# Attention in a five-phase kernel: the running maxima are split by GpSimd, transposed into score banks, copied out by ScalarE and added to the query rows by GpSimd

## What is computed

```
q = rope((layernorm(x) @ Wq.T + bq) per head)        # (4, 16, 512, 16)
k = rope((ctx @ Wk.T + bk) per head)
v = (ctx @ Wv.T + bv) per head
attn = softmax(einsum('bhld,bhkd->bhlk', q, k) * 16 ** -0.5, over k)
x = x + tanh(g_xattn[0]) * ((attn @ v) @ Wp.T + bp)
```

## Time and profile before

| | |
|---|---|
| median of 3 runs | 832.74 us (831.04 to 834.12) |
| the profiled execution's own time | 834.48 us |
| its span, first to last instruction | 832.7 us |
| mean granted TensorE clock | 0.932 |
| PE busy | 694.4 us (83%) |
| DVE busy | 475.5 us (57%) |
| ACT busy | 329.4 us (40%) |
| POOL busy | 245.0 us (29%) |
| first matmul of the attention passes to the start of the next phase | 109.3 to 328.0 us |

### The profile page before, as it was taken

The page is one execution under the profiler, slowest core; times in us unless marked ns, Lnnn a source line. Parts: engine busy times, 40 slices in busy tenths (PEclk is TensorE's granted clock), DMA queues, the critical chain, the costliest instruction groups (busy, mean ns, idle before and its releaser), DMA issues. The chain is left out here.

```text
span 832.7 us, 10715 instructions
## 1 busy us (share of the span) xinstructions
PE 694.4 (83%) x3613; PEld 413.5 (50%) x3632; DVE 475.5 (57%) x873; ACT 329.4 (40%) x584; POOL 245.0 (29%) x407
## 2 busy tenths in 40 slices
PE   3699869998998997855799999999488999975886
PEld 1377633333333332742455665656355767662554
DVE  3576668888888871643763113121437555456995
ACT  0167626677677676412341111141031120202565
POOL 2356530011011010353050001010103164347797
PEclk9699977999999999885899999999789998996999
DMA  5010000000000001930000000000100000000011
GB/s 186 13 32 25 13 7 0 2 1 0 1 1 1 1 1 71 394 155 0 1 1 0 1 1 0 0 0 1 13 1 0 1 1 1 1 0 0 20 38 45
DMA packets 14104, 21.45 MB, mean 26 GB/s; under 512 B 2160, under 2 KB 11504, under 8 KB 13296
## 3 DMA queue, kind: packets, MB, share of 16 engines
q1 hardware_dynamic: 13200, 20.34, 7.1%
q10 hardware_dynamic: 864, 0.59, 0.2%
HBM read 18.83 MB, written 2.10 MB: 25 GB/s over the span
## 5 line engine op out<-in xcount | busy, mean ns | idle before, releaser
L630 ACT ACTIVATE prob<-ps_s 128x512 f32<-128x512 f32 x256 | 133.9, 600 | 72.3 <-PE ps_s L518 71.6
L562 DVE TENSOR_REDUCE mx<-ps_f 128x2 f32<-128x1024 f32 x128 | 150.0, 1218 | 15.6 <-PE ps_f L498 8.1
L1038 DVE SCALAR_TENSOR_TENSOR qs<-ps_u,wmax,qs 128x512 f32<-128x512 f32 x40 | 29.7, 749 | 113.9 <-ACT qs L1000 113.8
L1000 ACT ACTIVATE qs<-ps_g,wmax 128x512 f32<-128x512 f32 x40 | 27.4, 687 | 144.1 <-PE ps_u L903 144.1
L916 PE MATMUL ps_yE<-down,qs 128*128 128x256 f32 x320 | 77.7, 387 | 7.9 <-DVE qs L1038 6.8
L518 PE MATMUL ps_s<-q_stacks,k_stacks 64*128 64x512 f32 x256 | 75.7, 425 | 10.2 <-ACT prob L630 9.1
L498 PE MATMUL ps_f<-k_stacks,q_stacks 64*128 64x512 f32 x256 | 64.9, 502 | 16.7 <-DVE q_stacks L581 9.7
L916 PEld LDWEIGHTS ps_yE<-down,qs 128*128 128x128 f32 x320 | 61.3, 193 | 22.0 <-DVE qs L1038 9.0
L527 PE MATMUL ps_o<-prob,vst 128*32 128x512 f32 x512 | 69.0, 612 | 0.0
L498 PEld LDWEIGHTS ps_f<-k_stacks,q_stacks 64*128 64x128 f32 x256 | 25.3, 194 | 72.7 <-issue 28.7
L599 POOL COPY vst<-va 128x272 f32<-128x272 f32 x16 | 6.8, 428 | 167.1 <-PE ps_o L527 167.1
(11 more groups left out here) (245 smaller groups left out, 1258.7 us busy)
## 6 DMA issues: line engine op xcount, KB each, us to landing
up<-in_up SPq DMA_DIRECT2D x10, 256.0 KB, 6.7
x<-in_x SPq DMA_DIRECT2D x4, 512.0 KB, 7.9
ctxT<-in_ctxT SPq DMA_DIRECT2D x16, 128.0 KB, 2.0
ks<-in_ctxTC SPq DMA_DIRECT2D x1, 2048.0 KB, 11.9
ks<-in_ctx SPq DMA_DIRECT2D x1, 2048.0 KB, 17.4
out<-x SPq DMA_DIRECT2D x16, 128.0 KB, 1.7
down<-in_down SPq DMA_DIRECT2D x1, 1280.0 KB, 5.7
ks<-in_wqv SPq DMA_DIRECT2D x1, 1024.0 KB, 20.7
```

Source lines behind the costliest of these rows:

```text
L562: dve.tensor_reduce(mx[:, f % 2, qt, 2 * pair:2 * pair + 2], ps_f[n % 2][:, :, :], AX_X, ALU.max).then_inc(used, 1)
L630: act.activation(prob[:, kt % 2, j, :], ps_s[n % 3][:, :], ACT.Exp, scale=SCALE)\
L1038: dve.scalar_tensor_tensor(out=h[:, k % 2, :], in0=ps_u[k % 2][:, :], scalar=wmax[:, 3, order[k], 1:2], in1=sg[:, k % 2, :], op0=ALU.mult, ...
```

## The change

Four things are changed together, all of them in `phase_attend`.

- The **split** of the maxima leaves VectorE's program and goes to GpSimd's, as three instructions for two (L576, L578 and L580 of the changed kernel). VectorE's program is now the 128 reductions and nothing else, and it no longer waits for the clearing of `mt`.
- The **transposes** go four by four, one half for each pair of heads, into banks of `ps_s` in place of a unit of `ps_f`. They take two places in the order of the score banks, ahead of scores 0 and of scores 2 in kt = 2 of the step before (they stood together at the head of kt = 3). The third bank back is now sometimes one of theirs.
- **ScalarE copies** each transposed half (128 x 512) out of its bank into the new tile `minus`, between its exponentials, and **GpSimd adds** it into the query rows (`lower`, L586, 128 x 512), two such additions per step in place of VectorE's single one.
- The first pass runs **14 units ahead** of the second in place of 12.

```
-def max_unit(f):
-    return UNITS + (UNITS + 1) * f + (MAX_AFTER if f < STEPS - 1 else 0)
+def score_slot(s, kt, j):
+    added = (0, 0, 1 + j // 2, 2)[kt] if s + 1 < STEPS else 0
+    return 2 + (QT * G + 2) * s + G * kt + j + added
+
+def max_slot(f, pair):
+    return score_slot(f - 1, 2, 2 * pair) - 1 if f else pair
...
# PE
-            def maxima(f):
-                n = max_unit(f)
+            def maxima(f, pair):
+                n = max_slot(f, pair)
                 pe.wait_ge(mt_ready, f + 1)
-                wait(pe, used, n - 1)
-                for pair in range(2):
-                    for qt in range(QT):
-                        last = pe.transpose(ps_f[n % 2][:, pair, qt * P:(qt + 1) * P], ...)
-                last.then_inc(filled, 1)
+                wait(pe, slot_read, n - 2)
+                for qt in range(QT):
+                    last = pe.transpose(ps_s[n % 3][:, qt * P:(qt + 1) * P], ...)
+                last.then_inc(slot_done, 1)
...
-            for i in range(UNITS):
-                first_scores(0, i)
-            for i in range(MAX_AFTER):
-                first_scores(1, i)
-            maxima(0)
-            for i in range(MAX_AFTER, 4):
-                first_scores(1, i)
+            for n in range(UNITS + 2):
+                first_scores(n)
+            for pair in range(2):
+                maxima(0, pair)
+            for n in range(UNITS + 2, LEAD):          # LEAD = 14
+                first_scores(n)
             for s in range(STEPS):
-                pe.wait_ge(used, max_unit(s) + 1)
+                pe.wait_ge(lowered, 2 * (s + 1))
                 for kt in range(QT):
-                    if kt == QT - 1 and s + 1 < STEPS:
-                        maxima(s + 1)
                     for half in range(2):
-                        f, i = ahead[2 * kt + half]
-                        if f < STEPS:
-                            first_scores(f, i)
+                        ahead = UNITS * s + LEAD + 2 * kt + half
+                        if ahead < UNITS * STEPS:
+                            first_scores(ahead)
+                        if kt == 2 and s + 1 < STEPS:
+                            maxima(s + 1, half)
                         for j in (2 * half, 2 * half + 1):
                             scores(s, kt, j)
...
# GpSimd
+            def split(f):
+                pool.wait_ge(used, UNITS * (f + 1))
+                ...
+                pool.tensor_scalar(high.bitcast(F32R), mx[:, f % 2, :, :], -1.0, None, ALU.mult).then_inc(mt_half, 1)
+                pool.wait_ge(mt_half, 2 * f + 1)
+                pool.tensor_tensor(low, mx[:, f % 2, :, :], high, ALU.add).then_inc(mt_half, 1)
+                pool.wait_ge(mt_half, 2 * f + 2)
+                pool.tensor_scalar(low, low, -1.0, None, ALU.mult).then_inc(mt_ready, 1)
+
+            def lower(f, pair):
+                pool.wait_ge(slot_read, max_slot(f, pair) + 1)
+                own = qs[:, 2 * f + pair, :]
+                pool.tensor_tensor(own, minus[:, pair, :], own.bitcast(F32), ALU.add).then_inc(lowered, 1)
...
             for s in range(STEPS):
                 if s > 1:
                     stage_values(s, s % 2)
+                if s + 1 < STEPS:
+                    split(s + 1)
+                    for pair in range(2):
+                        lower(s + 1, pair)
                 bias(s)
...
# ScalarE
+            def copy_maxima(f, pair):
+                n = max_slot(f, pair)
+                act.wait_ge(slot_done, n + 1)
+                wait(act, lowered, 2 * (f - 1) + pair + 1)
+                act.copy(minus[:, pair, :], ps_s[n % 3][:, :]).then_inc(slot_read, 1)
...
                 for j in range(G):
-                    n = s * 16 + kt * G + j
+                    n = score_slot(s, kt, j)
+                    if kt == 2 and j % 2 == 0 and s + 1 < STEPS:
+                        copy_maxima(s + 1, j // 2)
```

More of the change, by code:

```diff
@@ L478, in phase_attend @@
         filled, used = sem("filled"), sem("used")
-        mt_preset, mt_half, mt_ready = sem("mt_preset"), sem("mt_half"), sem("mt_ready")
-        s_done, exp_done, pv_done, o_copied = sem("s_done"), sem("exp_done"), sem("pv_done"), sem("o_copied")
+        mt_preset, mt_half, mt_ready, lowered = sem("mt_preset"), sem("mt_half"), sem("mt_ready"), sem("lowered")
+        slot_done, slot_read, pv_done, o_copied = sem("slot_done"), sem("slot_read"), sem("pv_done"), sem("o_copied")
         v_preset, v_ready = sem("v_preset"), sem("v_ready")
@@ L500, in first_scores @@
                 last.then_inc(filled, 1)
-            def maxima(f):
-                n = max_unit(f)
+            def maxima(f, pair):
+                n = max_slot(f, pair)
                 pe.wait_ge(mt_ready, f + 1)
-                wait(pe, used, n - 1)
-                for pair in range(2):
-                    for qt in range(QT):
-                        last = pe.transpose(ps_f[n % 2][:, pair, qt * P:(qt + 1) * P],
-                                            mt[:, f % 2, qt, 2 * pair:2 * pair + 2, :]
-                                            .rearrange("p h r -> p (h r)"), id32)
-                last.then_inc(filled, 1)
+                wait(pe, slot_read, n - 2)
+                for qt in range(QT):
+                    last = pe.transpose(ps_s[n % 3][:, qt * P:(qt + 1) * P],
+                                        mt[:, f % 2, qt, 2 * pair:2 * pair + 2, :]
+                                        .rearrange("p h r -> p (h r)"), id32)
+                last.then_inc(slot_done, 1)
             def scores(s, kt, j):
-                n = s * 16 + kt * G + j
-                wait(pe, exp_done, n - 2)
+                n = score_slot(s, kt, j)
+                wait(pe, slot_read, n - 2)
                 pair, h = divmod(j, 2)
                 pe.matmul(ps_s[n % 3][:, :], ks[rows(h), 2 * s + pair, kt * P:(kt + 1) * P],
-                          qs[rows(h), 2 * s + pair, :], start=True, stop=True).then_inc(s_done, 1)
+                          qs[rows(h), 2 * s + pair, :], start=True, stop=True).then_inc(slot_done, 1)
             def values(s, kt):
-                pe.wait_ge(exp_done, s * 16 + kt * G + G)
+                pe.wait_ge(slot_read, score_slot(s, kt, G - 1) + 1)
                 if kt == 0:
@@ L557, in _ @@
         def _(dve):
-            def first_maxima(f, i):
-                n = score_unit(f, i)
+            for n in range(UNITS * STEPS):
+                f, i = divmod(n, UNITS)
                 qt, pair = divmod(i, 2)
+                if i == 0:
+                    wait(dve, mt_ready, f - 1)
                 dve.wait_ge(filled, n + 1)
@@ L563, in first_maxima @@
                                   ALU.max).then_inc(used, 1)
[L565 to L589, removed]
         @block.gpsimd
@@ L616, in _ @@
             pool.wait_ge(bp_in, 16)
+            split(0)
+            for pair in range(2):
+                lower(0, pair)
             for s in range(STEPS):
@@ L623, in _ @@
         def _(act):
+            def copy_maxima(f, pair):
[3 more added lines that the diff above has]
+                act.copy(minus[:, pair, :], ps_s[n % 3][:, :]).then_inc(slot_read, 1)
             def exps(s, kt):
+                wait(act, pv_done, s * QT + kt - 1)
                 for j in range(G):
[L626 to L629, removed]
+                    n = score_slot(s, kt, j)
+                    if kt == 2 and j % 2 == 0 and s + 1 < STEPS:
+                        copy_maxima(s + 1, j // 2)
+                    act.wait_ge(slot_done, n + 1)
                     act.activation(prob[:, kt % 2, j, :], ps_s[n % 3][:, :], ACT.Exp, scale=SCALE)\
[L631 removed]
+                       .then_inc(slot_read, 1)
             def sums_out(s):
@@ L636, in sums_out @@
                 act.copy(o32[:, s, 0:S], ps_o[:, :]).then_inc(o_copied, 1)
+            for pair in range(2):
+                copy_maxima(0, pair)
             for s in range(STEPS):
```

16 lines of the change are left out of this document (8 added, 8 removed).

## The result

The changed kernel takes 838.74 us (median of 5 runs, 838.01 to 839.72) against 831.04 us (5 runs) for the kernel before beside it: a ratio of 1.0084, 95% interval 1.0061 to 1.0106. Run again later (9 runs, beside 20 of before) it gave 1.0069 (1.0047 to 1.0092). It is slower by 6 to 8 us, where 1.9 us faster was forecast, and 838.74 lies outside the range of 827.5 to 835.5.

The account below looks back on a forecast made before the run. It took a circle of waits between PE and ACT to bound the attention passes, with slack in DVE. 14 steps x -0.11, start -0.2 and end -0.2 gave -1.9 us: 830.9 us against 832.74, range 827.5 to 835.5.

Parts of the forecast that it names:

- The first exponential at 0.77 after the kt's start in ordinary kts: Ordinary kts: first exponential starts 0.77 us after the kt's start, within a kt of 2.84 (2.83 as a mean).
- kt = 2 at 3.96: The kt that receives the transposes lasts 3.96 us in place of 2.83, a cost of 1.13 a step.
- the 0.91 from the kt's start to the first copy: In kt = 2, ACT's first copy of transposes starts 0.86 to 0.96 us after the kt's start, taken as 0.91.
- the circle: PE and ACT waiting on each other in a kt: 0.77, 0.60, 0.05, 0.42 and 1.00, in sum 2.84 us.
- My upper end for this kt, 4.2: kt = 2 with long transpose latency and 0.1 us extra per change of matmul kind: 4.2, step 0.13 longer.
- kt = 3 as an ordinary kt, the gain of 1.24: kt = 3 loses its transposes and wait for DVE, falling from 4.07 to 2.83 us: 1.24 gained per step.
- GpSimd: Additions of 1.4 us each and a split of 0.9 stay off the path, 2.4 us to spare; lateness rival 0.06.
- VectorE's 19 us in 25: Attention passes: DVE's busy time in 25 us falls to near 19 from 21.70.
- The start, -0.2: Start of the attention passes: 1.26 us won by DVE's earlier start, 1.1 eaten by two units more: -0.2.
- The end, -0.2: Last step but one: kt = 1 and kt = 3 shorten, kt = 2 grows to 3.67; together -0.2 us.
- The sum: Whole kernel: 14 steps x -0.11 = -1.5, start -0.2, end -0.2: -1.9 us, forecast 830.9 us.
- the dearer transposes: Rival: transposes cost more between tiled matmuls, 0.13 to 0.4 a step, 833 to 838 us; chance 0.14.

Follow-up runs that it names:

- wait_order_undone: Changed kernel with ScalarE's old order of two waits before a block's first exponential (score first, values matmuls second); 1.0028 of the kernel before, step 12.68 us.
- wait_order_alone: Kernel before with only the order of two waits on ScalarE changed (values matmuls first, score second); 1.0021 of the kernel before, step 12.76 us.
- the two fillers: Changed kernel with a scratch clearing of 1024 or 2048 columns before each GpSimd addition; 1.0068 and 1.0420 of the kernel before.
- lead_12: Changed kernel with the first pass 12 units ahead in place of 14; 1.0176 of the kernel before, step 13.56 us.
- the long filler: Changed kernel with a scratch clearing of 2048 columns (1.81 us) before each GpSimd addition; 1.0420 of the kernel before, step 13.93 us.

## Why the prediction was wrong, point by point

- **The first exponential at 0.77 after the kt's start in ordinary kts, taken over to the changed kernel.** This is the step that failed first. I took kts 0, 1 and 3 to be as before because their matmuls are the same, and never weighed the moved `wait` line. The cost that I so put at nothing is 0.06 in each of them (2.89 and 2.90 for 2.83), 0.19 a step, and some 0.04 in kt = 2 (4.18 undone, 4.22 not). Runs wait_order_undone and wait_order_alone show it.
- **kt = 2 at 3.96.** The steps were right: the unit, the transposes, one copy and two exponentials, score 3 held by exponential 1. One term was too small, the 0.91 from the kt's start to the first copy. It measured 1.17: 0.05 more by the waits of the first point (1.13 with the order undone), 0.1 by the late entry of the transposes, and 0.1 because four of them can be read 0.69 after their start, where I had 0.52 to 0.62. I had taken 0.51 for four, half of 1.03, off the 1.13 of eight. The prediction says that this 1.03 has no change between the two kinds of matmul in it. It has one: eight at the 0.109 us from one transpose to the next make 0.87, and some 0.15 more goes until the next matmul. Four fewer save 0.44, and 1.13 - 0.44 = 0.69. The rest of the circle held: 4.22 - 1.17 = 3.05, where 3.96 - 0.91 = 3.05 was forecast. My upper end for this kt, 4.2, is close to the 4.22, but by luck in part: it was made of two late changes between the kinds of matmul, where one was in the circle, and the waits weren't in it.
- **kt = 3 as an ordinary kt, the gain of 1.24.** Right in its mechanism: it is 2.90 in place of 4.07, a gain of 1.17, and 2.83 to 2.85 without the first point.
- **GpSimd.** Right: 1.27 for 1.4 forecast, a margin of 2.5 us for 2.4, shown by the two fillers. The split took 0.96 with its signals (207.54 to 208.50), for 0.9. None of the 32 additions stood longer beside VectorE's reductions (1262 to 1280 ns).
- **VectorE's 19 us in 25.** Right, 19.03, and no gain from it.
- **The start, -0.2.** It was +0.14 (17.85 for 17.71 from first matmul to first score). VectorE began 0.54 after the first matmul as forecast. The two units more cost 2.2 us, by lead_12, where I had 1.1; the rest of the start came out 2.1 better than before, where I had 1.26. In the whole, 12 units are worse.
- **The end, -0.2.** It was +0.3, by the same two points as the steps.
- **The sum.** -0.11 a step was forecast, +0.35 measured: 0.19 for the waits in three kts and 0.26 in kt = 2 make 0.45 of the 0.46 between them. The rival nearest to it, the dearer transposes at 833 to 838 with 0.14, had the mechanism of 0.1 of this; the 0.19 stood nowhere. The range went by the terms one at a time, and its upper end left no room for a term that I hadn't seen.

## What to carry to other kernels

Before the terms are counted, find the circle of waits that sets the period, and then price every line of the diff that touches an instruction in it, down to the order of two waits: 0.06 us in three blocks of a step was 0.2 of its 12.6 us here. Of several waits ahead of an instruction, write first the one that is satisfied last, and look in the trace at which wait stands alone. Work that is taken from an engine with slack brings nothing by its size, only by a wait for it that goes. Where transposes must go into a loop of narrower matmuls, try them together and first in the block, so that what waits for them starts early.

## What the runs showed of the hardware that I had not expected

- A wait as an instruction of its own on ScalarE, when it is the one that comes last, puts the start of the next activation 0.06 us later (0.49 in place of 0.43 from the score matmul's start to the exponential's); one that is satisfied early costs nothing to see.
- A group of four 128 x 128 transposes between 64-row matmuls takes 0.56 to 0.58 to the next matmul and enters 0.1 late; eight behind the values matmuls take 1.02 to 1.03 in all.
- GpSimd's addition of 128x512 with the rounded type as its output takes 1.27 us, the same as with plain float output in the earlier trace rows, in all 32 turns (1262 to 1280 ns) beside VectorE's reductions.
- With PE idle for 0.93 us more at the head of every step (the long filler) the clock of the stretch fell to 0.95, 0.98 and 0.93 of full in places where it is 1.00 in the changed kernel (the two levels, 2.4 and 1.2 GHz, mixed), and its four runs had mean clocks of 0.901 to 0.925 against 0.926 to 0.929 for the changed kernel. That the hole is what brought the clock down now and then is my reading of it; no run here shows it alone.
